# A quantised two-layer network whose first-layer sums are half kept in SBUF, rounded through fp16, and computed in blocks of two groups

## The reference, cut to what matters

```
def quant_act_uint8(x):
    s = max(max(x), EPS) / 255
    return clip(round(x / s), 0, 255) * s, s
h = relu(quant_linear(x, w1, b1))      # x: 4096 x 256, w1: 1024 x 256
out = x1 + quant_linear(h, w2, b2)     # w2: 256 x 1024
```

## Time and profile before

| | us |
|---|---|
| median of 3 runs | 1224.04 |
| lowest, highest | 1218.09, 1226.12 |
| the profiled execution | 1214.47 |
| its span, first to last instruction | 1212.6 |

### The profile page before, as it was taken

How to read it: one execution, slowest core, us unless ns; L and a number is a source line. 1 busy time by engine, 2 the same in 40 slices (tenths; PEclk the granted TensorE clock), 3 DMA queues, 4 the chain that set the end, 5 groups by cost and what they waited for, 6 DMA issues and landing times.

```text
span 1212.6 us, 29895 instructions
## 1 busy us (share of the span) xinstructions
PE 994.3 (82%) x9726; PEld 764.8 (63%) x9727; DVE 797.0 (66%) x2823; ACT 533.3 (44%) x1750; POOL 373.3 (31%) x414
## 2 busy tenths in 40 slices
PE   6777777777776999999999999664739867796898
PEld 5556666656565888888888887533405644463365
DVE  5676777766775868985655555454605755568988
ACT  4555555555554333333333333443204444434286
POOL 1002112111113566333333332155550555521000
PEclk7555555555556999999999999877859999898999
DMA  8213323223233468554434433552442778771024
GB/s 238 93 59 101 96 85 102 88 88 102 77 104 105 84 133 171 102 84 67 65 60 61 62 57 64 169 193 80 136 124 62 204 204 213 195 256 59 1 35 105
DMA packets 139299, 132.91 MB, mean 110 GB/s; under 512 B 80770, under 2 KB 114307, under 8 KB 138979
## 3 DMA queue, kind: packets, MB, share of 16 engines
q1 hardware_dynamic: 118050, 91.49, 29.0%
q0 software_dynamic: 21120, 39.77, 14.4%
HBM read 68.91 MB, written 56.87 MB: 104 GB/s over the span
## 4 chain that ended last, share of the span: by engine, by line
PE 55%; DVE 16%; issue 11%; ACT 9%; DMA 4%; another core or an unknown queue 2%; POOL 2%; SPq 0%; DVEq 0%; POOLq 0%; ACTq 0%
PE ps L1561 15%; PE ps L1571 14%; PE ps L2208 7%; PE ps L766 7%; DVE ps L2135 5%; PE ps L2213 4%; ACT work L2059 4%; ACT ps L2054 3%; PE ps L1321 2%; DVE imax L1412 2%; PE ps L1326 2%; POOL mresults L1498 2%; PE ps L2178 1%; PE ps L1292 1%
## 5 line engine op out<-in xcount | busy, mean ns | idle before, releaser
L1590 ACT ACTIVATE lane<-ps,b_now 128x256 f32<-128x256 f32 (+1 forms) x312 | 141.0, 455 | 248.6 <-PE ps L1561 231.6
L1561 PE MATMUL ps<-lane,W 128*128 128x256 f16 (+1 forms) x1872 | 204.6, 265 | 3.6 <-issue 2.3
L1571 PE MATMUL ps<-W,lane 128*128 x1704 | 192.8, 273 | 1.0 <-DVE lane L1669 0.8
L1561 PEld LDWEIGHTS ps<-lane,W 128*128 x1872 | 173.8, 98 | 30.4 <-issue 7.2
L1571 PEld LDWEIGHTS ps<-W,lane 128*128 128x128 f16 x1704 | 165.4, 98 | 22.5 <-issue 2.1
L1751 POOL DMA_INDIRECT results<-lane,dest x71 | 114.1, 1607 | 202.7 <-DVE lane L1655 156.3
L2208 PE MATMUL ps<-work 128*128 128x16 f16 x2048 | 98.9, 177 | 89.4 <-ACT work L2059 88.8
L2208 PEld LDWEIGHTS ps<-work 128*128 128x128 f16 x2048 | 76.1, 106 | 141.1 <-ACT work L2059 139.8
L1669 DVE TENSOR_TENSOR lane<-lane 128x256 f16<-128x256 f32 (+1 forms) x312 | 125.7, 403 | 10.8
L766 PE MATMUL ps<-W,work 128*128 128x512 f16 x384 | 101.3, 413 | 17.5 <-issue 16.7
L1721 POOL DMA_INDIRECT rows<-work,slot_of x64 | 63.4, 990 | 156.4 <-DVE ps L2135 152.4
(11 more groups left out here) (285 smaller groups left out, 1626.5 us busy)
## 6 DMA issues: line engine op xcount, KB each, us to landing
stage<-rweights SPq DMA_DIRECT2D x39, 256.0 KB
stage<-in_w1T SPq DMA_DIRECT2D x16, 512.0 KB, 3.9
stage<-in_w2T SPq DMA_DIRECT2D x16, 512.0 KB, 4.0
b_now<-in_b SPq DMA_DIRECT2D x39, 128.0 KB
W<-mrows SPq DMA_DIRECT2D x16, 260.0 KB
work<-in_zT SPq DMA_DIRECT2D x32, 128.0 KB, 2.2
results<-in_xn SPq DMA_DIRECT2D x32, 128.0 KB
W<-results SPq DMA_DIRECT2D x16, 256.0 KB, 3.7
```

Of the source, the lines that this page charges most:

```text
L1561: last = pe.matmul(ps[:, f % 4, 0:wide], of_e(W1[:, bass.ds(e, 1), a, k, f * P:(f + 1) * P]), xrows[:, b, k], start=(i == 0 and k == 0), s ...
L1571: last = pe.matmul(ps[:, 4 + q, 0:D], hid[:, a, f, q * P:(q + 1) * P], of_e(W2[:, bass.ds(e, 1), b, f]), start=(i == 0 and f == 0), stop=( ...
L1590: act.activation(v4[:, f % 4, 0:wide], ps[:, f % 4, 0:wide], ACT.Relu, bias=b1_now[:, p, f:f + 1], scale=A_SCALE / W_SCALE).then_inc(l1_v, 1)
```

## The change

Everything before the last stage stays as it is, but for where some buffers of the last stage lie. In the last stage:

- **Rounding.** Adding 1024 to a value of 0 to 255 and writing it as fp16 leaves it rounded; `max(1024)` and `subtract 1024` then give relu and the integer, as bfloat16. ACT's output becomes fp16 and 128x1024 where a block has two groups. The second step is a DVE `tensor_scalar` with fp16 input and bfloat16 output in place. Of the input, DVE now does both steps for the first four positions; for the other four ACT and POOL share them.
- **Pass 1.** PSUM has three pairs of banks for the 32 units, in an order that mixes two pairs of groups. For half of the units ACT copies the sums to SBUF (`held_sums`, 128x1024 float32) and DVE takes the maximum of the copy.
- **Pass 2.** It goes in blocks: groups (0, 2), (1, 3), (4, 6), then 5, then 7. Blocks (0, 2) and (4, 6) read the held sums, so that PE computes sums again for groups 1, 3, 5 and 7 only.
- **x+bias** of the last four groups moves from DVE to POOL.
- The matmuls for the weight scales (`diag`) and the copy of `rs2` move ahead of pass 1, and PE's first two sums of block (1, 3) ahead of `largest(1)`.

```diff
+BY_POSITION = (0, 2, 1, 3, 4, 6, 5, 7)
+BLOCKS = ((0, 2), (1, 3), (4, 6), (5,), (7,))
+HELD_SUMS = (0, None, 1, None, None)
+OUT_BANK = (4, 4, 4, 4, 6)
+ROUND16 = 1024.0
+    order = [(0, 0), (0, 1)]
+    for f in range(2, FC):
+        order += [(0, f), (1, f - 2)]
+    order += [(2, 0), (1, FC - 2), (2, 1), (1, FC - 1)]
+    for f in range(2, FC):
+        order += [(2, f), (3, f - 2)]
+    return order + [(3, FC - 2), (3, FC - 1)]
+TRANSPOSES_AT = {0: 2, 1: 3, 8: 4, 10: 5, 12: 6, 14: 7}
+QUANTISED_HERE = 4
+QUANTISED_AT = {2: 5, 4: 6, 6: 7}
...
+            for f in range(2):
+                hidden(1, f)
             largest(1)
+            for i in range(len(BLOCKS)):
+                for f in range(FC):
+                    if i == 2 and f < 4:
+                        hidden(3, f)
+                    for a in ahead(i, f):
+                        hidden(*a)
+                    output(i, f)
...
+            def quantised(p):
+                g = BY_POSITION[p]
+                act.activation(yq16[:, p], y[:, GT * g:GT * g + GT].rearrange("p q d -> p (q d)"), ACT.Relu,
+                               scale=inv[:, 0:1], bias=round16[:]).then_inc(yq_m, 1)
+            act.wait_ge(inv_ready, 1)
+            quantised(QUANTISED_HERE)
+            for p in range(2):
+                transposed(p)
+            for u, (n, f) in enumerate(SUM_UNITS):
+                if u in QUANTISED_AT:
+                    quantised(QUANTISED_AT[u])
+                if is_held(n):
+                    act.wait_ge(ia_ps, u + 1)
+                    act.activation(held_sums[n // 2][f], banks(u), ACT.Copy).then_inc(ia_held, 1)
+                if u in TRANSPOSES_AT:
+                    transposed(TRANSPOSES_AT[u])
...
+            def quantised(p):
+                g = BY_POSITION[p]
+                link(dve, dve.tensor_scalar(yq16[:, p], y[:, GT * g:GT * g + GT].rearrange("p q d -> p (q d)"),
+                                            inv[:, 0:1], ROUND16, ALU.mult, ALU.add))
+                dve.tensor_scalar(yq[:, p], yq16[:, p], ROUND16, ROUND16, ALU.max, ALU.subtract).then_inc(yq_n, 1)
...
+            def hidden(i, f):
+                n = len(BLOCKS[i]) * GN
+                dve.wait_ge(hb_h, FC * i + f + 1)
+                dve.tensor_scalar(V[i % 2][:, f, 0:n], V16[i % 2][:, f, 0:n], ROUND16, ROUND16, ALU.max, ALU.subtract)\
+                   .then_inc(hb_qd, 1)
...
+            for f in range(FC):
+                hidden(0, f)
+                if f == 1:
...
+                    round_bias(dve, bq2, rs2, vs[:, 0, 0:D]).then_inc(bq_ready, 1)
...
+            for i in range(1, len(BLOCKS)):
+                halves = 2 * len(BLOCKS[i - 1])
                 for f in range(FC):
+                    if 2 * f < halves:
+                        scaled(i - 1, 2 * f)
+                        scaled(i - 1, 2 * f + 1)
+                    elif f - halves // 2 < halves:
+                        added(i - 1, f - halves // 2)
+                    hidden(i, f)
+            for h in range(2):
+                scaled(len(BLOCKS) - 1, h)
+                added(len(BLOCKS) - 1, h)
...
+            for p in range(QUANTISED_HERE, GROUPS):
+                pool.wait_ge(yq_m, p - QUANTISED_HERE + 1)
+                pool.tensor_scalar(yq[:, p], yq16[:, p], ROUND16, ROUND16, ALU.max, ALU.subtract).then_inc(yq_p, 1)
+            pool.wait_ge(bq_ready, 3)
+            for g in range(ADDED, GROUPS):
+                xg_ = x1[:, GT * g:GT * g + GT]
+                pool.tensor_tensor(xg_, xg_, bq2.rearrange("p (a d) -> p a d", a=1).broadcast_to([P, GT, D]), ALU.add)\
+                    .then_inc(xb_ready, 1)
```

More of the change, by code:

```diff
@@ L1280, in transposes, with sums @@
                 last.then_inc(yq_ps, 1)
[L1282 to L1297, removed]
+            def sums(u):
+                n, f = SUM_UNITS[u]
+                if u == 2:
+                    pe.wait_ge(wt_cp, 5)
+                if u >= 3:
+                    if is_held(SUM_UNITS[u - 3][0]):
+                        pe.wait_ge(ia_held, held_upto(u - 2))
+                    else:
+                        pe.wait_ge(ia_mx, u - 2)
+                for m in range(2):
+                    if f == 0:
+                        pe.wait_ge(yq_T, 2 * n + m + 1)
+                    for k in range(DC):
+                        last = pe.matmul(ps[:, 2 * (u % 3) + m], w1qT[:, k, f * P:(f + 1) * P],
+                                         yqT[:, k, (2 * n + m) * GN:(2 * n + m + 1) * GN],
+                                         start=(k == 0), stop=(k == DC - 1))
+                last.then_inc(ia_ps, 1)
@@ L1313, in ffn_pe @@
             last.then_inc(wt_ps, 1)
-            largest(1)
[L1315 to L1348, removed]
@@ L1350, in ffn_pe @@
-            for f in range(FC):
-                hidden(0, f)
-            ffn_groups(pe, group)
+            largest(0)
+            for p in range(2):
+                transposes(p)
+            for u in range(len(SUM_UNITS)):
+                sums(u)
+                if u in TRANSPOSES_AT:
+                    transposes(TRANSPOSES_AT[u])
+            hidden_users = {b: ("sums", len(SUM_UNITS) - 1 + b // 2) for b in range(4)}
+            out_users = {}
+            at = {"hidden": 0, "halves": 0}
@@ new lines, in hidden @@
+            def hidden(i, f):
+                width = len(BLOCKS[i])
+                first = at["hidden"] % 4
+                at["hidden"] += width
+                for b in range(first, first + width):
+                    kind, n = hidden_users[b]
+                    pe.wait_ge(ia_mx if kind == "sums" else hb_h, n)
+                    hidden_users[b] = ("block", FC * i + f + 1)
+                for m in range(width):
+                    p = POSITION[BLOCKS[i][m]]
+                    for k in range(DC):
+                        last = pe.matmul(ps[:, first + m], w1qT[:, k, f * P:(f + 1) * P],
+                                         yqT[:, k, GN * p:GN * (p + 1)], start=(k == 0), stop=(k == DC - 1))
+                last.then_inc(hb_ps, 1)
```

235 lines of the change are left out of this document (125 added, 110 removed).

## The result

| | before | after |
|---|---|---|
| median of 20 runs each, us | 1221.95 | 1224.91 |
| lowest, highest | 1217.43, 1226.15 | 1220.22, 1230.63 |
| profiled execution, its span | 1214.47, 1212.6 | 1224.08, 1221.5 |

The ratio is 1.0033, 95% interval [1.0018, 1.0049]: the change costs 4.0 us [2.2, 6.0]; the two medians alone differ by 3.0. The time stayed within 1%, as the 0.78 said, and inside the range, but it moved the other way.

The account below looks back on a forecast made before the run. Pass 1 was taken as bound by DVE's reductions, pass 2 by PE. The terms 0.7 + 1.6 + 0.1 - 5.9 = -3.5 us, from the median 1224.04, gave 1220.5 us, range 1210 to 1233.

Parts of the forecast that it names:

- the 0.78: Whole kernel: the chance given that the time stays within 1%, 12 us, of the kernel before.
- its sum for pass 2: Pass 2, from its release: blocks and tail summed to 54.5 us against 60.45, a gain of 5.9 us.
- The case: Rival, start and first two blocks: POOL and DVE hinder each other, DVE waits, +2 to +9 us; chance 0.20.
- the rival: Rival, DVE's rounding: 0.43 us per 1024 columns; start gains 0.5 us, blocks 2.8, total -6.8; chance 0.22.
- the slow rounding: Start and pass 2: DVE's new rounding of 1024 columns taken as 0.69 us, by the float32 row.
- The term that had been set to nothing: Pass 2: x+bias on POOL, 4 x 1.22 us off DVE already left out of the sums, no cost added.
- The start: Start of pass 1, from the known `inv` to the first reduction: 0.7 us longer than before.
- Pass 1: The 32 reductions: 37.8 us in place of 38.7, plus a hole of 2.5 us: +1.6 us.
- the sign: Release of pass 2: the second scale released 51.6 to 52 us after the reduction of `ymax`, before 49.2.
- the case on the other side: Rival, pass 1: POOL's four roundings slow, up to 14 us each, whole kernel 1250 to 1264 us; chance 0.09.
- PE's low clock: Start of pass 1: four us more at the 1.2 GHz level cost 1.5 to 2 us; in the range only.
- PE's 13.8 us: Pass 2: the change takes 32 x 0.43 = 13.8 us from PE; ACT, then DVE, take up more than half.

Follow-up runs that it names:

- e1: The changed kernel with GpSimd's four additions of x+bias left out, so part of the result is missing; ratio to the kernel before 0.9964.
- e2: The changed kernel with x+bias back on VectorE, behind the last four roundings of block (1, 3); ratio to the kernel before 0.9960.
- e7: The changed kernel with x+bias spread over VectorE, GpSimd's roundings after VectorE's, and ScalarE's three late input roundings one unit later; ratio to the kernel before 0.9948.
- e3: The changed kernel with GpSimd's first rounding waiting until VectorE has rounded its four positions; ratio to the kernel before 0.9998.
- e9: The changed kernel with GpSimd's x+bias held back until all eight roundings of block (0, 2) are done; ratio to the kernel before 0.9989.
- e8: e7 plus the second bias's rounding cut into its five instructions, one after each of five roundings of block (0, 2); ratio to the kernel before 0.9926.
- e6: The changed kernel with GpSimd's four x+bias additions of 1024 columns cut into sixteen of 256; ratio to the kernel before 0.9993.
- e4: The kernel before with only the four x+bias additions moved from VectorE to GpSimd; ratio to the kernel before 1.0097.

## Why the prediction was wrong

**The step that failed** is a sentence of its sum for pass 2: "x+bias on POOL takes 4 x 1.22 us from DVE, already left out of these sums; it has some 30 us until its first use." It asked when the additions had to be done and whether POOL had time for them. It did not ask what stood on DVE meanwhile. They cost 5.3 us in the first block (e1), more than the 4.9 us of DVE's time that they had been, of which only 0.6 us lengthen pass 2's second block when DVE has them there (e2), and next to nothing when they are spread (e7). The case stood among the rivals with 0.20 and with the right place ("which starts just when DVE has six roundings to catch up"). What kept it small was reading as POOL's loss only. There DVE ran a float32 addition of two SBUF operands for 1.22 us, of unchanged length, and it had begun first (1083.42, POOL 1083.61). That two engines collide in one row was no evidence on which of them would wait in another, where POOL's instruction is under way first.

**Its price** was bounded by one to four waits of 1.04 to 2.4 us. Measured: the four additions, of 2.5 us each, lengthen six roundings by 8.1 us (10.70 - 6 x 0.43), of which 5.3 reach the end of the block, and the start loses 0.7: 6.0 together, inside the +2 to +9.

**The rounding**, 0.69 us by the row of the float32 input, took 0.43: the rival's value. The 3.3 us that the rival worked out from it did not show. Without the collision the first reduction still starts at 8.6 us (e3), as forecast with the slow rounding, and pass 2 takes 54.6 us (e1) against the 54.5 forecast. That agreement is luck: in e1 the blocks behind the first are 1.0 us shorter than forecast, and the first is 1.1 longer, with PE's clock at 0.50; where the clock was higher it was 1.0 shorter (e2, e9: 11.5 against 12.5). In the sum of the trace, then, the start is 1.0 over the forecast, pass 1 from there to the release 1.3 under it, and pass 2 5.4 over it: from -3.5 to about +1.5. The term that had been set to nothing is the one that turned the sign.

**The start** came at +1.75 in place of +0.7: 0.7 of the excess is the same collision on a smaller scale, 0.3 the two slower matmuls before it (e3). **Pass 1** took 39.1 us from its first reduction, where 40.3 were predicted (37.8 and the hole of 2.5): the holes are as large as forecast, but the reductions are 1.13 us apart instead of 1.18. **The release** at 51.3 fell just under the 51.6 to 52 named as the sign. **POOL's rounding** at 3.6 us stayed below the 6 us from which PE would have waited for it, and the case on the other side fell away.

**Pass 2's other blocks** were right within 0.6 us each. PE's low clock had been named for the start alone and not for pass 2. The reason given for PE's 13.8 us not coming through, that ACT and then DVE bound the blocks, held for the first one. In after's chain each later block begins with DVE's scalings and is then PE's nearly to its end, in (4, 6) and 5 too, for which DVE had been forecast.

**Not settled:** why the ratio of after lies 2.5 us above what its traced stage gives (the two medians lie 1.5 above it); the other executions may spend more in the sparse block, where the clock varies, and no run shows it. How much the clock costs by itself was not measured apart from what makes PE wait.

## What to carry to other kernels

When work is moved from VectorE to GpSimd, look first at what VectorE will run beside it. If that is a queue of quick SBUF-to-SBUF instructions on which TensorE waits, each pays up to the length of one GpSimd instruction, and the move can cost more than it frees. Put such work where VectorE reads PSUM or has pauses, cut it small, or leave it on VectorE, spread over places where it has time; in this study that last was the fastest (e7, e8). That it could also lie beside VectorE's reductions is not shown for additions. And a mean that is far above what the same operation costs on half the columns hides a collision; the timeline shows with whom.

## What the runs showed of the hardware

**VectorE and GpSimd take turns.** Beside GpSimd's float32 additions, a rounding (`tensor_scalar`, fp16 to bfloat16 in SBUF) or a cast from bytes waits until the running addition is over. A rounding of 0.43 us then takes 2.57 with additions of 1024 columns (after) and 0.95 with 256 (e6); the profile counts that wait in the duration of VectorE's instruction. GpSimd's additions hardly grow: 2.35 us for the first one of e9, beside which VectorE starts no rounding, against 2.52 in after. `tensor_tensor` with one operand in PSUM doesn't wait (0.68 us in e4). With both operands in SBUF it does (2.82 us in e4, 2.83 in e9). Beside POOL's rounding, reductions keep their 1.21 us, from SBUF and from PSUM; no trace here has a reduction beside an addition of POOL.

The Trainium skill (SBUF — State Buffer, "Who interferes with whom") calls it an exclusive lock on ports that the two engines share, held for the whole instruction by the one that issues first, with an exemption for VectorE's reductions and for instructions with at most one SBUF input outside its two-port modes. For the additions the traces agree, as far as they go. For GpSimd's rounding they don't: within its 4.40 us three of VectorE's roundings took 1.14, 0.43 and 1.13, so that VectorE was not shut out for 4.4 us at a time; the measurement decides, and how long it is shut out there was not tried.

**The rate of the rounding** with 16-bit input and output in SBUF is 0.43 us for 1024 columns, 0.36 from one start to the next, against 0.75 us for the first step, which reads float32 (L1489). The Trainium skill (VectorE: DVE Perf Modes, "The perf-mode tier table") gives `tensor_scalar` twice the rate in the first case; the trace comes near it, at 1.7 times (0.75 / 0.43).

**GpSimd** needs 3.63 us for the same rounding, 8.4 times as long, and 1.04 for a cast from bytes of that size.
